# Fences on landings ahead of GpSimd's indirect transfers in a routed-experts and recurrence kernel

## What is computed

```python
# layer 0: shared expert and two of eight routed experts for each token
shared = silu(xf @ w1) * (xf @ w3) @ w2
s = sigmoid(concat([xf, tf]) @ router_W)
topk_idx = top_k(s + router_bias, 2)          # gates: the two s, normalized to sum 1
routed = sum over the two of gate * (gelu(xf @ W1e[e]) @ W2e[e])
x = x + (shared + routed) / 3
# layer 1: gated recurrence over the 256 steps, all 32 rows at once
gate = sigmoid(h @ Wh.T + z_t @ Wz.T + b)
h = tanh(h * (1 - alpha) + gate * z_t)
x = x + h at every step
```

## Time and profile before

| | |
|---|---|
| timed runs (3), median | 1001.31 us |
| lowest to highest | 998.25 to 1001.55 us |
| profiled execution, span from first to last instruction | 1155.6 us |
| profiled execution, its own time beside the span | not in the records |
| mean granted TensorE clock in it | 0.879 |
| busy: TensorE matmul, VectorE, ScalarE, GpSimd | 79%, 62%, 45%, 24% of the span |
| indirect scatters and gathers | 128 and 128 |

### The profile page before, as it was taken

One profiled execution on the slowest core, in us unless ns is written; L12 is line 12 of the kernel. 1 busy time (PEld: TensorE's weight loads), 2 busy tenths in 40 slices (PEclk: granted clock), 3 DMA queues, 4 the chain that ended last, 5 costly groups with the idle time before them and its releaser, 6 DMA issues.

```text
span 1155.6 us, 29134 instructions
## 1 busy us (share of the span) xinstructions
PE 910.9 (79%) x9550; PEld 633.8 (55%) x9550; DVE 716.7 (62%) x2491; ACT 516.3 (45%) x1431; POOL 275.5 (24%) x318
## 2 busy tenths in 40 slices
PE   2178769976999589986899779995999859998653
PEld 2067338843687247852588336862578426874432
DVE  5246447855777287754778457773878547657754
ACT  3155226632475145732466225742467324653333
POOL 1500730056002530045100550035300560005000
PEclk7599979987999789987999879996899879999955
DMA  7782323332243222532233322532223322322010
GB/s 239 246 256 78 124 73 93 112 108 75 72 130 124 88 66 72 142 100 78 81 102 103 115 69 65 145 114 83 73 66 111 107 77 75 106 88 74 10 29 19
DMA packets 91746, 115.24 MB, mean 100 GB/s; under 512 B 10930, under 2 KB 81108, under 8 KB 91604
## 3 DMA queue, kind: packets, MB, share of 16 engines
q1 hardware_dynamic: 77028, 73.43, 22.0%
q0 software_dynamic: 13856, 39.86, 10.7%
q10 hardware_dynamic: 720, 0.05, 0.1%
HBM read 56.68 MB, written 56.62 MB: 98 GB/s over the span
## 4 chain that ended last, share of the span: by engine, by line
PE 40%; DVE 16%; another core or an unknown queue 16%; ACT 10%; issue 10%; DMA 5%; POOL 2%; SPq 1%; DVEq 0%; ACTq 0%; POOLq 0%
PE bank L1127 36%; DVE pre L974 3%; PE bank L1250 3%; DVE hid_low L919 3%; DMA x_pair<-x_slots_even 3%; DMA x_pair<-x_slots_odd 2%; POOL x_slots_even L547 1%; DVE prod L906 1%; DVE zr L961 1%; ACT hid_high L674 1%; SPq L427 1%; ACT th L685 1%; DVE hs_low L981 1%; ACT hist L696 1%
## 5 line engine op out<-in xcount | busy, mean ns | idle before, releaser
L974 DVE TENSOR_TENSOR_SCAN pre<-th,zr 128x128 f32<-128x128 f32 x256 | 108.3, 423 | 232.2 <-ACT th L685 220.1
L1127 PE MATMUL bank<-hs_high,gwt_high 128*128 128x32 f16 x1024 | 81.2, 181 | 119.6 <-ACT hs_high L695 96.9
L685 ACT ACTIVATE th<-bank 128x64 f32<-128x64 f32 x256 | 59.5, 232 | 255.2 <-remote 164.6
L529 POOL TENSOR_TENSOR fence_pool<-zeros 128x1 f32<-128x1 f32 x48 | 12.3, 256 | 673.4 <-DVE is_low L869 353.5
L1127 PE MATMUL bank<-xe_high,w1e_high 128*128 128x128 f16 x768 | 161.3, 227 | 5.2 <-DVE xe_low L892 2.7
L1127 PEld LDWEIGHTS bank<-hs_high,gwt_high 128*128 128x128 f16 x1024 | 65.9, 100 | 171.7 <-ACT hs_high L695 125.7
L1127 PE MATMUL bank<-xe_low,w1e_high 128*128 128x128 f16 x768 | 159.3, 221 | 0.9 <-issue 0.9
L1127 PE MATMUL bank<-xe_high,w1e_low 128*128 128x128 f16 x768 | 158.9, 220 | 0.2
L695 ACT ACTIVATE hs_high<-pre 128x64 f16<-128x64 f32 x256 | 66.5, 260 | 188.0 <-DVE pre L974 176.8
L1127 PE MATMUL bank<-xs_high,w_high 128*128 128x512 f16 x256 | 109.6, 428 | 20.4 <-DVE prod L906 19.9
L1127 PE MATMUL bank<-xs_low,w_high 128*128 128x512 f16 x256 | 110.3, 431 | 2.8 <-issue 2.8
(11 more groups left out here) (162 smaller groups left out, 2307.4 us busy)
## 6 DMA issues: line engine op xcount, KB each, us to landing
x_pair<-x_slots_even SPq DMA_DIRECT2D x48, 256.0 KB
y_slots_even<-y_pair SPq DMA_DIRECT2D x48, 256.0 KB
x_pair<-x_slots_odd SPq DMA_DIRECT2D x48, 256.0 KB
y_slots_odd<-y_pair SPq DMA_DIRECT2D x48, 256.0 KB
x_tok<-in_x_dram SPq DMA_DIRECT2D x32, 256.0 KB, 5.3
out_dram<-o_tok SPq DMA_DIRECT2D x128, 64.0 KB, 1.7
x_slots_even<-zeros POOLq DMA_DIRECT2D x1, 3072.0 KB, 14.9
x_slots_odd<-zeros POOLq DMA_DIRECT2D x1, 3072.0 KB, 12.5
```

What stands on the lines that cost most here:

```text
L529: nc.gpsimd.tensor_tensor(fence_pool[:], zeros[:, 0:1], zeros[:, 1:2], ALU.mult).then_inc(s_fence, 1)
L685: nc.scalar.activation(flat3(th[:, s % 2, :, :, 1]), gate_sums(s), ACT.Tanh, scale=0.5 / UP).then_inc(s_th, 1)
L974: dve.tensor_tensor_scan(every(pre[:, s % 2]), every(th[:, s % 2]), every(zr[:, s % 2]), 0.0, ALU.mult, ALU.add).then_inc(s_pre, 1)
L1127: return pe.matmul(out_ap, w, mov, start=start, stop=stop, skip_group_check=True)
```

## The change

Ahead of the transfers of a token tile GpSimd now waits for the landing of earlier ones. A wait is `pass_landed`: a wait for the landing semaphore, a wait for the count of such fences so far, and a 128x1 multiply that counts up `s_land`. For a scatter of tile j >= 2 the landing is that of tile j - 2, told apart by two semaphores for even and odd tiles, on both of which SP now waits with half the count. For a gather of tile j with j % 4 > 0 it is that of tile j - 1. There are 6 waits at the scatters of a section and 6 at its gathers, beside the fences that were there.

```diff
--- before.py
+++ after.py
@@ -147,6 +147,7 @@
         left = sb("left", [P, NJ, 16])
         fence = sb("fence", [P, 1])
         fence_pool = sb("fence_pool", [P, 1])
+        fence_land = sb("fence_land", [P, 1])
         mask = sb("mask", [P, NJ, E])
         mask16 = sb("mask16", [P, NJ, E], F16)
         smask = sb("smask", [P, NJ, E])
@@ -270,8 +271,9 @@
         s_rk = sem("s_rk")
         s_chain = sem("s_chain")
         s_placed = sem("s_placed")
-        s_scat = sem("s_scat")
+        s_scat = [sem("s_scat_even"), sem("s_scat_odd")]
         s_fence = sem("s_fence")
+        s_land = sem("s_land")
         s_och = sem("s_och")
         s_turno = sem("s_turno")
         s_otok = sem("s_otok")
@@ -444,7 +446,8 @@
 
             def next_section(b):
 
-                sp.wait_ge(s_scat, (b.g + 2) * (16 * TOPK * NJ))
+                for half in range(2):
+                    sp.wait_ge(s_scat[half], (b.g + 2) * (8 * TOPK * NJ))
                 for p in range(NIN):
                     if b.n >= 0:
                         sp.wait_ge(s_xt, b.g * NPAIR + NPAIR - NIN + p + 1)
@@ -539,16 +542,33 @@
                 if b.n == 0:
                     pool.wait_ge(s_zero[1], 16)
                 pass_fence(b.g * FENCES + 1)
-                scatter_tiles(par, range(0, SCAT_FIRST))
-
-            def scatter_tiles(par, tiles):
+                scatter_tiles(b.g, par, range(0, SCAT_FIRST))
+
+            PASSES = 2 * (NJ - 2)
+
+            def pass_landed(landed, count, passed):
+
+                pool.wait_ge(landed, count)
+                pool.wait_ge(s_land, passed)
+                nc.gpsimd.tensor_tensor(fence_land[:], zeros[:, 0:1], zeros[:, 1:2], ALU.mult).then_inc(s_land, 1)
+
+            def scatter_tiles(g, par, tiles):
+
+                section = 0 if g is None else g + 1
                 for j in tiles:
+                    if j >= 2:
+                        passed = 1 if g is None else 1 + (NJ - 2) + g * PASSES + (NYG - 1 if tiles[0] > 0 else 0)
+                        pass_landed(s_scat[j % 2], section * (8 * TOPK * NJ) + j // 2 * (16 * TOPK), passed + j - 2)
                     for k in range(TOPK):
                         pool.indirect_dma_start(x_slots[par], at_slots(x_slots, par, j, k), x_tok[:, par, j, :], None
-                                                ).then_inc(s_scat, 16)
+                                                ).then_inc(s_scat[j % 2], 16)
 
             def gather(b, j):
                 par = b.n % 2
+                if j % NYG > 0:
+                    scattered = (SCAT_FIRST - 2 if j < NYG else NJ - 2) if b.prep else 0
+                    pass_landed(s_got[j % NYG - 1], (b.g * 2 + j // NYG + 1) * (16 * TOPK),
+                                1 + (NJ - 2) + b.g * PASSES + scattered + j - 1 - j // NYG)
                 for k in range(TOPK):
                     pool.indirect_dma_start(y_got[:, j % NYG, k, :], None, y_slots[par], at_slots(y_slots, par, j, k)
                                             ).then_inc(s_got[j % NYG], 16)
@@ -567,7 +587,7 @@
                     for j in range(NYG):
                         gather(b, j)
                     if b.prep:
-                        scatter_tiles((b.n + 1) % 2, range(SCAT_FIRST, NJ))
+                        scatter_tiles(b.g, (b.n + 1) % 2, range(SCAT_FIRST, NJ))
                     for j in range(NYG, NJ):
                         pool.wait_ge(s_r, b.g * NJ + j - NYG + 1)
                         pass_fence(b.g * FENCES + 3 + j - NYG)
@@ -577,7 +597,8 @@
             pool.wait_ge(s_zero[0], 16)
             pool.wait_ge(s_chain, SLOT_LINK)
             nc.gpsimd.tensor_tensor(fence_pool[:], zeros[:, 0:1], zeros[:, 1:2], ALU.mult).then_inc(s_fence, 1)
-            scatter_tiles(0, range(NJ))
+            nc.gpsimd.tensor_tensor(fence_land[:], zeros[:, 0:1], zeros[:, 1:2], ALU.mult).then_inc(s_land, 1)
+            scatter_tiles(None, 0, range(NJ))
             pool.wait_ge(s_up, 3)
             clear_slots(1)
             run_bodies(pool, body)
```

## The result

| | before | after |
|---|---|---|
| timed, median | 1000.43 us (4 runs, 998.25 to 1001.55) | 1048.52 us (4 runs, 1044.72 to 1052.57) |
| profiled execution | span 1155.6 us, another lot of runs | 1052.57 us, span 1050.8 |

A forecast was written before the change was run, and what follows sets the result against it. With "remote" waits taken as the profile's own, gathers reach VectorE barely in time; exposed landings add 6.2 (n = 0) + 18.6 (n = 1 to 6) + 3.2 (n = 7) = 28.0 us to 1001.3, giving 1029.3, range 985 to 1054.

The forecast's parts named there:

- "remote" waits: ScalarE's tanh instructions waiting for a TensorE semaphore, for something the trace calls "remote"; read as 188.1 us of the profiled span.
- main reading of the profile: Most "remote" waits belong to the profiled execution alone, explaining why it is at least 154 us longer than a timed one.
- 3.1 us to spare at tile 3: Without "remote" waits, section n = 2's tile 3 lands at 390.3 and VectorE wants it at 393.4, before the change.
- 967.5 us: Profiled span 1155.6 less 188.1 of "remote" waits; leaves 33.8 us of the timed run around the span or in remaining waits.
- A gather tile: GpSimd's gathers: each waiting tile costs 4.40 us instead of 2.52, so three cost 5.6 us more.
- Sections 1 to 6: Tile 3's gather lands 3.1 us late for VectorE and the recurrence in each of six sections, 18.6 us.
- the scatter fences: GpSimd's fences at scatters, 0.2 us each: three ahead of the first gathers add 0.6 us, three behind 0.6.
- Section 0: First section, n = 0: tile 3 is late already without the change, so all 6.2 us count.
- Prologue: Ahead of the first scatters: one fence, one semaphore reset and SP's wait have no waiter, 0.2 us or less, taken as 0.
- (a): Rival, hidden: "remote" waits are in timed runs too, so no gather of tile 3 is late; 1001 us, chance 0.2.
- (c): Rival, fully bound: GpSimd already bounds every section, so 6.2 us count in all eight; 1051 us, chance 0.1.
- (b): Rival, faster: unbroken rows of transfers cause "remote" waits, and the change breaks them; 986 us, chance 0.2.

The follow-up runs named there:

- e6: Against the kernel before, only the waits ahead of the gathers of tiles 5 to 7: 1003.4 us beside 1000.2 on chip 8, ratio 1.0034.
- e7: The kernel before with SCAT_FIRST = 4 instead of 5, one scatter tile less ahead of the first gathers, no added waits: 1002.7 us beside 1000.2 on chip 8.
- e5: The whole change run again against the kernel before, on chip 8: 1044.8 us beside 1000.2, ratio 1.0449.
- e10: Against the kernel before, only the waits ahead of gathers of tiles 1 to 3 and 5 to 7: 1035.0 us beside 1000.5 on chip 4.
- e11: Against the kernel before, waits at the bodies' scatters and gathers of tiles 1 to 3, none in the prologue: 1041.3 us beside 1000.5 on chip 4.
- e2: Against the kernel before, only the six scatter waits in the prologue: 1169.4 us beside 1163.0 on chip 9, ratio 1.0055.
- e1: Against the kernel before, all added fences but without the wait for a landing: 1153.3 us beside 1163.0 on chip 9, ratio 0.9927.
- e8: Against the kernel before, only the waits ahead of the gathers of tiles 1 to 3: 1155.4 us beside 1164.3 on chip 7, ratio 0.9936.
- e9: The whole change against the kernel before, on chip 7: 1110.1 us beside 1164.3, ratio 0.9540.

## Why the prediction came out as it did

The direction, the range and the mechanism held: exposed landings make the gathers of tiles 2 and 3 late, and the recurrence behind them pays. The size was short by 20 us, 28 against 48, and its main reading of the profile, that the "remote" waits belong to the profiled execution alone, was wrong. By its own steps:

**What bounds the kernel.** Taking the "remote" waits out of the profile was the right basis for these timed runs: the traces of chips 4 and 8 have none, and the predicted 3.1 us to spare at tile 3 are 3.2 in e6. That these two agree is in part luck. From the first gather to the take of tile 3 there are 15.6 us in e6 and 14.4 in the forecast; the row of gathers is 0.7 and the landing 0.45 us longer than in it. Nor are 967.5 us the span without these waits: on chips 4 and 8 the kernel before spans 995.6 to 999.9 us, so of the 33.8 us 2.1 lie around the span, and the subtraction took out some 30 us too much. The reason given for it was wrong. The waits do not belong to profiling: on chips 7, 9 and 11 the profiled execution shows them and takes no longer than the other timed runs. What was read as profile against timed run was most likely chip against chip; the chip of that profile is not on record.

**A gather tile.** Predicted 4.40 us, measured 5.10 in n = 2. The term that was off is the one from the second transfer to the fence, put at the y store's 2.46 and measured at 2.87 to 3.42 (up to 5.24 at the gathers of tiles 4 to 7: issue at 396.35, fence at 401.59). Scatters of equal size were the nearest row and still too short. By the Trainium skill ("DMA: Bandwidth & Descriptors", section "Anatomy of one DMA — SWDGE (gpsimd) path") the estimate for 128 KB was 2.3 us, with most of it completion; this case's gathers of n = 2, from issue to fence, are 0.6 to 1.1 us above that, so the measurement decides. How much of it is completion, no run here shows.

**Sections 1 to 6.** Predicted 3.1 us each. Against e7, which is the kernel before but for one scatter tile, e5's sections 1 to 5 are longer by 3.3, 3.7, 6.6, 3.0 and 3.4 us (differences of the starts of the first fences), and from section 6 to the end by 6.2. That is 26.2 against 21.8 predicted for n = 1 to 7. For n = 2 the sum can be redone: a tile took 2.74 us before (e6) and 5.10 after, three of them make 7.1, and less the 3.2 to spare 3.9 are left, with 3.7 measured. So the gathers cost 7.1 us where 5.6 were predicted, and the scatter fences, put at 0.6, cost nothing here: the ten scatters end at the same time as the y stores land, with or without them (first fence of the section to gather fence 14.4 us in e6 and 363.37 - 348.77 = 14.6 in the changed kernel). Section 3, where `r_part` waits 4.2 us for tile 3, makes most of the excess. Two things are there in e5's trace. The second gather of tile 3 is issued after 2.01 us of idle time behind the first instead of 0.3:

```profile
492.72 0.95 POOL L573 DMA_INDIRECT y_got<-y_slots_odd,where  x1 [2.01 <-issue]
```

The traces of the result and of e10 and e11 have this gap at the same place, e6 and e7 do not; its cause is open. Then, after a stretch of 5 us with TensorE busy for 2.6, it is granted 0.65 to 0.66 of its clock from 495 to 505, so for most of that time the lower of its two levels, and it is busy for 108.8 us in this section against 104.7 in e7, where the granted clock is 1.00 throughout. Over the whole span it is busy for 870.2 us in e5 and 854.6 in e7. A lower clock behind the longer waits is thus part of the cost, for which the forecast has no term.

**Section 0.** Predicted 6.2, measured 12.8 (101.7 in e7, 114.5 in e5). The step that failed is the working for tiles 4 to 7, done for n = 2 only, where they are hidden. In section 0 no recurrence runs between, VectorE asks for them earlier, and they are late as well: 4.28 us at tile 6 and 1.43 at tile 7 in e5, beside 3.55 at tile 3. In e11, which has no waits there, section 0 is 105.8 us long (first fences at 114.11 and 219.86). So the waits ahead of tiles 1 to 3 cost 4.1 of the 12.8 us, less than the 6.2 predicted, and the missing term some 8.7.

**Prologue.** Predicted 0, as "places without a waiter" counted only the fence and SP's wait; the six scatter waits of the prologue were not costed at all. "The wait never holds" was taken from a scatter of body 0, with 2.45 us from issue to landing. In the prologue tile 0's second transfer is issued at 28.86 and lets its fence go at 37.19, 8.3 us later, 3.87 of them waited for, and SP's first load and what follows stand behind it: 6.4 us alone (e2); the first load is 7.0 us later in the trace after than in the one before, and 5.3 between e6 and e5, on one chip.

In the traces of e5 and e7 section 0 starts 7.5 us apart (118.28 and 110.83). These 7.5, the 6.6 missed in section 0 and the 4.4 missed behind it make, unrounded, 18.4; with the 28.0 predicted that is 46.4, the difference of the two spans (1042.4 - 996.0). It closes because all terms are read from the same two traces, and it says where the time lies, to within a few us: e7's profiled execution is the fastest of its ten (998.1, median 1002.7), by medians the change costs 44.6 us on this chip, and without the prologue's waits section 0 starts anywhere from 110.8 (e7) to 114.1 (e11).

**The rivals.** (a) Hidden did not occur on a chip of this kind. (c) "GpSimd bounds every section" is nearest in time, 1051, but not in kind: in sections 1 to 7 of the result's trace tiles 0 and 1 are never late (in e5's, tile 1 once, by 0.31 us), and e6 and e7 have no late tile there at all, so GpSimd did not bound these sections before. (b) holds on other chips, in part: on chip 7 the change is 4.6% faster. Its reason needs mending: not unbroken rows as such (e1), but transfers issued without waiting for a landing. Its forecast that the profile would shrink by 100 us without the timed run following most likely compared two chips; on one chip, span and time differ by 1.7 to 2.1 us.

**What stays open.** What a TensorE semaphore waits for behind GpSimd's transfers on some chips. By the Trainium skill ("Perfetto Trace Analysis", section "Tensor Engine Instruction") it goes out once PSUM acknowledges the write, and the trace has only an estimated end; no run here shows which of the two is late. Waiting for a landing also spreads the gathers, from 2.5 to 5.1 us a tile; whether the same pace without the wait would do away with the "remote" waits was not run. Each chip was used in one lot only, so that the waits come with the chip, and not with something else that differed between the lots, is not shown. Nor was any run with the first gathers' waits alone had on a chip without these waits.

## What to carry to other kernels

When a profiled span and the timed runs differ by far more than the 2 us that lie around the span here, compare them on one chip before calling the difference the profiler's. A wait for the transfer just before turns the issue period of 2.5 us a tile into issue plus landing, 5.1; work out the slack of each taker, in every section with another rhythm and in the prologue, not in the typical one alone. A guard for a stall that only some chips have can be worth 5% there and cost 5% elsewhere.

## What the runs showed of the hardware

On chips 7, 9 and 11 ScalarE, and at times VectorE, waited for TensorE up to 14 us with no event in the trace that ended the wait, around rows of GpSimd's indirect transfers (e8: 13.64 us), in each traced run there; on chips 4 and 8 in none. The kernel before took 16% longer there (1163 against 1000). Small instructions between the transfers did not help (e1, 186.8 us of such waits); waiting for landings halved them (e9, 92.7 us).

In the trace after, from the issue of a gather of 128 rows of 1 KB to the fence that its landing let go, there were 2.7 to 5.2 us where the fence had to wait for it; a scatter of the same size had 2.45 us at most in body 0 and 8.3 us in the prologue.
